# The last tile's y read straight from four PSUM banks, and the integers of the tile before it made by ScalarE alone

## The chip, the cores and the metric

One core of one Trainium2 chip runs the kernel. The metric is device microseconds of one execution. The kernel before took 420.11 us (median of 3 runs, 419.92 to 420.31). One execution was also recorded by the hardware profiler.

## The reference, cut to what matters

2048 tokens of 512 values pass through two residual blocks. The first sends each token through one of four expert MLPs. The second, with which this case deals, is a BitNet feed-forward layer: activations are rounded to 8-bit integers with one scale per token, weights are -1, 0 or 1, and a Hadamard transform stands before the down projection.

```
def act_quant(x):                       # per token: scale from the largest |x| of its row
    scale = 128 / clip(max(|x|, axis=-1), 1e-5)
    return clip(round(x * scale), -128, 127) / scale
gate, up = bitlinear(x, w_gate), bitlinear(x, w_up)
intermediate = silu(gate) * up          # 2048 values per token
y = fwht(intermediate)                  # Hadamard transform of the 2048 values
x = x + tanh(g) * bitlinear(y, w_down)  # y goes through act_quant first
```

The scale of a token needs the maximum over its whole row of y, so no integer of y can be made before the last part of that row is there.

## The kernel before, in words

The tokens form 16 tiles of 128 (NT = 16). A tile's 2048 values of y are worked on in NQ = 4 quarters of 512, one PSUM bank each. For one tile the steps are:

- gate and up products on TensorE, silu on ScalarE, their product on VectorE;
- four butterfly levels on VectorE (lines 1201 and 1209), which leave `mixed`;
- per quarter: four transposes on TensorE (line 427), ScalarE copies them from PSUM into `mT` (`mT_evacuate`, line 836), four Hadamard products on TensorE (line 588) leave y in a bank, ScalarE copies it into the SBUF tensor `y` (`y_evacuate`, line 841);
- VectorE takes the maximum of |y| and from it the scale `yqs`;
- integers: ScalarE writes `y8` (int8, which rounds) and widens it into `yq` (bf16); lines 824 and 829 in the loop, `end_integers` (892 and 896) at the end. VectorE can do the same in two passes (`y_integers`, lines 1364 and 1367);
- the DMA queue of SyncE (SP) transposes each quarter of `yq` into `yqT` (`turn_y`, lines 279 to 284), TensorE multiplies it by the down weights (line 595), VectorE scales and adds the residual (`finish`, line 1309), and GpSimd (POOL) writes the tile to the output by an indirect DMA (line 410).

The work on a tile is spread over several rounds of a loop. What remains after the loop is in a function `drain` on each engine, with an order written out by hand. It calls the last four tiles Z, A, B and C (12 to 15). In this text "B1" is quarter 1 of tile B, and so on. SP, POOL and the compute engines run in order, and each waits on semaphores that the others count up.

In the drain before: B's integers come half from VectorE (quarters 0 and 1, counted by `yq_end_set`) and half from ScalarE (2 and 3, counted by `yq_end_act`). C's four Hadamard quarters go in turn to the two banks `end_had`, and each waits until ScalarE has copied an earlier y out of its bank; VectorE then takes C's maximum quarter by quarter from SBUF (line 1410). C's integers are made by VectorE (0 and 2) and ScalarE (1 and 3). C's quarters are not transposed by DMA but by TensorE (`y_transposes`, line 693, called T0 to T3 here), and copied to `yT_end` by VectorE (line 1419) and ScalarE (line 935). TensorE's order at the end is C's Hadamards, A1, A2, A3, B0, B1, T0, T1, B2, T2, B3, T3, and the 16 products of C (line 681). A quarter of B can be transposed into `yqT` only after the product of the same quarter of A has read it:

```
sp.wait_ge(down_done, (t - 1) * NQ + (m + 1))
```

Of the kernel before, what the change touches and what calls it, by code (L numbers as in the profile page):

```python
# [22 lines left out]
ALU = mybir.AluOpType  # L23
ACT = mybir.ActivationFunctionType
# [7 lines left out]
NT = T // P  # L32
# [43 lines left out]
def gated_moe_bitnet_kernel(nc, x, ids, ctxt, wgate, wup, wdown, gates, consts, out):  # L76
    with ExitStack() as persistent:
# [123 lines left out]
        end_had = (ps_had, ps_up[0])  # L201
        first_h, first_xT = (ps_h, bank[4]), (ps_xT, bank[5])
        first_gate, first_up = (bank[7], bank[4]), (bank[5], bank[6])
        ps_down_last, ps_yT = bank[0], (bank[2], bank[5], bank[3], bank[4])


        in_ids, in_small, in_gate = sem("in_ids"), sem("in_small"), sem("in_gate")
# [39 lines left out]
        @block.sync  # L247
        def _(sp):
            sp.dma_start(idt[:, :], ids).then_inc(in_ids, 16)
            sp.dma_start(cst[:, 0:C_RANK], consts[:, 0:C_RANK]).then_inc(in_rank, 16)  # L250
            sp.dma_start(cst[:, C_RANK:C_N], consts[:, C_RANK:C_N]).then_inc(in_small, 16)
            sp.dma_start(gate_in[:, :], gates).then_inc(in_gate, 16)
            for e in range(E):
                if e == E - 1:
                    sp.wait_ge(gathered[1], 16)
                sp.dma_start(stage[:, e, :], ctxt[:, e, :]).then_inc(in_slot[e], 16)

            for w in range(3):
                for c in range(4):
                    if w == 0:  # L260
                        sp.wait_ge(ct_lo_set, c + 1)
                        sp.wait_ge(h_done, FIRST)
                    else:
                        sp.wait_ge(wround_set, 4 * (w - 1) + c + 1)
                    sp.dma_start(stage[:, c, :], W_DRAM[w][:, c, :]).then_inc(in_slot[c], 16)

            sp.wait_ge(wround_set, 9)

            def turn_x(t):
                sp.wait_ge(xq_set, t + 1)  # L270
                if t >= 1:
                    sp.wait_ge(gate_done, NQ * (t - 1) + 1)
                if t >= 2:
                    sp.wait_ge(up_done, NQ * (t - 1))
                sp.dma_start_transpose(xqT[:, t % 2, :, :], xq[:, t % 2, :]).then_inc(xqT_set, 16)

            def turn_y(t, m):
                if t == NT - 2:
                    sp.wait_ge((yq_end_set, yq_end_act)[m // 2], m % 2 + 1)
                else:  # L280
                    sp.wait_ge(yq_set, t * NQ + (m + 1))
                if t >= 1:
                    sp.wait_ge(down_done, (t - 1) * NQ + (m + 1))
                sp.dma_start_transpose(yqT[:, m, :, :], yq[:, t % 2, 512 * m:512 * (m + 1)]).then_inc(yqT_set[m], 16)

            turn_x(0)
            for t in range(NT + 1):
                if t == 3:
                    turn_x(4)
                if t >= 4:  # L290
                    turn_y(t - 4, 3)
                if t >= 3:
                    turn_y(t - 3, 0)
                    turn_y(t - 3, 1)
                if t != 3 and t + 1 < NT:
                    turn_x(t + 1)
                if t >= 3:
                    turn_y(t - 3, 2)
            turn_y(NT - 3, 3)
            for m in range(NQ):  # L300
                turn_y(NT - 2, m)
# [122 lines left out]
        def _(pe):  # L424
# [207 lines left out]
            def drain():  # L632

                Z, A, B, C = NT - 4, NT - 3, NT - 2, NT - 1

                def mix(n):
                    if n >= 2:
                        pe.wait_ge(mT_set, B * NQ + n - 1)
                    mix_transposes(B, B % 2, n)

                def had_b(n):
                    pe.wait_ge(y_set, B * NQ + n - 1)
                    hadamard(B, n, end_had[n % 2])

                mix(0)
                mix(1)
                down_product_int(Z, Z % 2, 1)
                had_b(0)
                down_product_int(Z, Z % 2, 2)
                had_b(1)  # L650
                mix(2)
                mix(3)
                down_product_int(Z, Z % 2, 3)
                had_b(2)
                had_b(3)
                pe.wait_ge(res_set, A - 1)
                down_product_int(A, A % 2, 0)
                for n in range(2):
                    pe.wait_ge(mT_set, B * NQ + n + 3)
                    last_transposes(n)  # L660
                for n in range(NQ):
                    pe.wait_ge(y_set, B * NQ + n + 3)
                    hadamard(C, n, end_had[n % 2])
                    if n < 2:
                        last_transposes(n + 2)
                for m in range(1, NQ):
                    down_product_int(A, A % 2, m)
                pe.wait_ge(res_set, B - 1)
                down_product_int(B, B % 2, 0)
                down_product_int(B, B % 2, 1)  # L670
                y_transposes(0)
                y_transposes(1)
                down_product_int(B, B % 2, 2)
                y_transposes(2)
                down_product_int(B, B % 2, 3)
                y_transposes(3)
                for m in range(NQ):
                    pe.wait_ge((yT_dve_set, yT_act_set)[m % 2], m // 2 + 1)
                    for g in range(4):
                        block_ = (m + 2) % NQ * 4 + g  # L680
                        last = nc.tensor.matmul(ps_down_last[:, :], yT_end[:, m, g, :],  # L681
                                                wq[:, 2, block_ * D:(block_ + 1) * D],
                                                start=(m == 0 and g == 0), stop=(m == 3 and g == 3))
                last.then_inc(down_done, NQ)

            def y_transposes(m):

                if m == 0:
                    pe.wait_ge(ident_set, 1)
                pe.wait_ge((yq_end_set, yq_end_act)[m % 2], 2 + m // 2 + 1)  # L690
                for g in range(4):
                    cols = slice(512 * m + g * P, 512 * m + (g + 1) * P)
                    last = nc.tensor.matmul(ps_yT[m][:, g * P:(g + 1) * P], yq[:, (NT - 1) % 2, cols], ident_bf[:, :],
                                            start=True, stop=True)
                last.then_inc(yT_done, 1)
# [14 lines left out]
        def _(act_e):  # L710
# [172 lines left out]
            def end_integers(t, m, i):  # L883

                b = t % 2
                if i % 2 == 0:
                    act_e.wait_ge(yqs_set, t + 1)
                if i < 2:
                    act_e.wait_ge(yq_set, (NT - 2) * NQ)
                else:  # L890
                    act_e.wait_ge(yq_end_act, i - 1)
                nc.scalar.activation(y8[:, i % 2, :], y[:, b, 512 * m:512 * (m + 1)], ACT.Copy,
                                     scale=yqs[:, b:b + 1]).then_inc(yround_set, 1)
                act_e.wait_ge(yround_set, (NT - 2) * NQ + i + 1)
                act_e.wait_ge(yqT_set[m], t * 16 - 16)
# [3 lines left out]
            def drain():  # L899
# [20 lines left out]
                mT_evacuate(C, 0)  # L920
                mT_evacuate(C, 1)
                integers(A, 3)
                y_evacuate(C, C % 2, 0, end_had[0])
                mT_evacuate(C, 2)
                y_evacuate(C, C % 2, 1, end_had[1])
                mT_evacuate(C, 3)
                end_integers(B, 2, 0)
                y_evacuate(C, C % 2, 2, end_had[0])
                end_integers(B, 3, 1)
                y_evacuate(C, C % 2, 3, end_had[1])  # L930
                end_integers(C, 1, 2)
                end_integers(C, 3, 3)
                for m in (1, 3):
                    act_e.wait_ge(yT_done, m + 1)
                    nc.scalar.activation(yT_end[:, m, :, :].rearrange("p g t -> p (g t)"), ps_yT[m][:, :],
# [15 lines left out]
        def _(dve):  # L951
# [409 lines left out]
            def y_integers(t, b, m):  # L1361

                quarter = y[:, b, 512 * m:512 * (m + 1)]
                st.did(ts(quarter, quarter, yqs[:, b:b + 1], MAGIC, ALU.mult, ALU.add))
                st.wait()
                dve.wait_ge(yqT_set[m], t * 16 - 16)
                ts(yq[:, b, 512 * m:512 * (m + 1)], quarter, MAGIC, QB - 1, ALU.subtract,
                   ALU.min).then_inc(yq_end_set, 1)
# [11 lines left out]
            def drain():  # L1380
# [19 lines left out]
                y_max(B, B % 2, 0, (0, 2), st)  # L1400
                step = y_max(B, B % 2, 1, (2, 4), st)
                end_scales(B, step, 2)
                dve.wait_ge(yqs_set, B + 1)
                for m in range(2):
                    y_integers(B, B % 2, m)
                finish(Z, Z % 2)
                for p in range(NQ):
                    dve.wait_ge(y_set, C * NQ + p + 1)
                    n = p
                    step = st.did(nc.vector.tensor_reduce(ymax_part[:, c, p:p + 1], y[:, c, 512 * n:512 * (n + 1)],  # L1410
                                                          AX_X, ALU.max, apply_absolute_value=True))
                end_scales(C, step, NQ)
                dve.wait_ge(yqs_set, C + 1)
                for m in (0, 2):
                    y_integers(C, c, m)
                finish(A, A % 2)
                for m in (0, 2):
# [97 lines left out]
```

## Time and profile before

| what | value |
|---|---|
| median of 3 runs | 420.11 us (419.92 to 420.31) |
| the profiled execution | 419.76 us, of which the span 417.8 us |
| TensorE matmul busy | 388.4 us (93% of the span) |
| VectorE busy | 365.6 us (88%) |
| ScalarE busy | 291.3 us (70%) |
| granted TensorE clock, mean | 0.995 |

The span goes from the first to the last instruction; 1.96 us of the profiled execution lie around it. The shares are means over stages with different limits. The change touches only the drain, which starts at about 380 us of the span, so what matters is who waits for whom between 390 and 411 us.

### The profile page before, as it was taken

Reading aid. Unit: us, or ns where it says so; the run is one execution under the profiler, and the core shown is the slowest. Engines: PE = TensorE matmul, PEld = TensorE weight load, DVE = VectorE, ACT = ScalarE, POOL = GpSimd, SP = SyncE. Lnnn points to the kernel's source line nnn. Section 1 sums busy time; section 2 is a strip of 40 time slices with the busy share of each in tenths; the row PEclk is TensorE's granted clock in tenths of the full one; section 3 lists DMA queues with packets and bytes.
Section 4 is the critical chain, followed back from the end, with each engine's and each line's share of the span. In section 5 each row is a group of like instructions: output and inputs, shape, how many; then the busy total and the mean of one; then the engine's idle time right before and its main releaser. Section 6 shows DMA issues by size and latency. Waiting matters only on the chain.

```text
span 417.8 us, 7359 instructions
## 1 busy us (share of the span) xinstructions
PE 388.4 (93%) x2170; PEld 270.2 (65%) x2203; DVE 365.6 (88%) x653; ACT 291.3 (70%) x450; POOL 175.3 (42%) x207
## 2 busy tenths in 40 slices
PE   1899999999999989989999999999999999999891
PEld 1347788888887564756666666666666666667740
DVE  6788587779888889999999999999999999998970
ACT  4446686587875243658888888888888888877960
POOL 0667310114124111053575575575575575522021
PEclk9999999999999999999999999999999999999997
DMA  7759474065000000235155155155155155255241
GB/s 244 268 160 417 154 247 157 1 211 192 2 15 0 13 14 8 57 63 103 44 109 126 44 107 126 44 107 126 43 107 126 43 107 126 48 106 113 50 102 50
DMA packets 48969, 43.66 MB, mean 105 GB/s; under 512 B 42673, under 2 KB 42801, under 8 KB 46897
## 3 DMA queue, kind: packets, MB, share of 16 engines
q1 hardware_dynamic: 44224, 27.11, 22.6%
q0 software_dynamic: 4720, 16.26, 16.5%
q8 instruction: 13, 0.21, 0.2%
q14 instruction: 12, 0.09, 0.1%
HBM read 21.33 MB, written 4.19 MB: 61 GB/s over the span
## 4 chain that ended last, share of the span: by engine, by line
PE 78%; DVE 11%; issue 5%; DMA 3%; ACT 2%; POOL 1%; DVEq 0%; SPq 0%; POOLq 0%; ACTq 0%
PE bank L465 21%; PE bank L588 13%; PE bank L595 11%; PE bank L564 10%; PE bank L571 10%; PE bank L427 9%; DVE prod L1182 2%; DVE ct_lo L972 1%; DMA xs<-x_dram,order 1%; PE bank L532 1%; DMA yqT<-yq 1%; PE bank L681 1%; DVE bfly L1209 1%; DVE mixed L1209 1%; DVE xs L1100 1%
## 5 line engine op out<-in xcount | busy, mean ns | idle before, releaser
L588 PEld LDWEIGHTS bank<-cst,mT 128*128 128x128 f32 x512 | 66.5, 191 | 12.9 <-issue 2.1
L588 PE MATMUL bank<-cst,mT 128*128 128x128 f32 x512 | 67.7, 276 | 3.4 <-ACT mT L836 3.4
L571 PE MATMUL bank<-wq,xqT 128*128 128x512 bf16 x232 | 61.0, 379 | 0.4
L595 PE MATMUL bank<-wq,yqT 128*128 128x512 bf16 x227 | 59.3, 379 | 1.6 <-DMA yqT<-yq 0.8
L564 PE MATMUL bank<-wq,xqT 128*128 128x512 bf16 x231 | 59.8, 379 | 0.5
L836 ACT ACTIVATE mT<-bank 128x512 f32<-128x512 f32 x64 | 37.6, 592 | 17.9 <-PE bank L427 17.9
L410 POOL DMA_INDIRECT out_dram<-res,order x16 | 19.4, 1215 | 70.4 <-DVE res L1309 70.4
L824 ACT ACTIVATE y<-y,yqs 128x512 int8<-128x512 f32 x56 | 40.2, 718 | 11.8 <-POOL yqs L368 11.8
L841 ACT ACTIVATE y<-bank 128x512 f32<-128x512 f32 x64 | 37.6, 588 | 9.7 <-PE bank L588 9.5
L861 ACT ACTIVATE sg<-bank,gate_s 128x512 f32<-128x512 f32 x60 | 41.0, 683 | 4.1 <-PE bank L564 3.9
L1182 DVE TENSOR_TENSOR prod<-bank,sg 128x512 f32<-128x512 f32 x64 | 43.3, 677 | 0.6 <-ACT sg L861 0.5
L571 PEld LDWEIGHTS bank<-wq,xqT 128*128 128x128 bf16 x240 | 23.5, 98 | 28.3
L427 PE MATMUL bank<-cst,mixed 128*128 128x128 f32 x256 | 37.9, 273 | 0.5 <-DVE mixed L1201 0.5
L427 PEld LDWEIGHTS bank<-cst,mixed 128*128 128x128 f32 x256 | 31.4, 141 | 10.5 <-issue 0.9
L1288 DVE TENSOR_REDUCE ymax_part<-y 128x1 f32<-128x1024 f32 x30 | 36.3, 1212 | 2.1 <-ACT y L841 1.0
L1209 DVE TENSOR_TENSOR mixed<-prod 128x1024 f32<-128x1024 f32 x32 | 37.8, 1219 | 0.1
L366 POOL TENSOR_SCALAR out_s<-yamax,down_c 128x1 f32<-128x1 f32 x13 | 29.7, 2282 | 19.3 <-DVE yamax L1299 19.3
L1209 DVE TENSOR_TENSOR prod<-bfly 128x1024 f32<-128x1024 f32 x30 | 36.0, 1211 | 0.0
L829 ACT ACTIVATE yq<-y 128x512 bf16<-128x512 int8 x56 | 35.3, 630 | 0.6
L1209 DVE TENSOR_TENSOR bfly<-prod 128x1024 f32<-128x1024 f32 x30 | 35.3, 1216 | 0.0
L595 PEld LDWEIGHTS bank<-wq,yqT 128*128 128x128 bf16 x240 | 23.2, 98 | 17.3 <-DMA yqT<-yq 1.5
L564 PEld LDWEIGHTS bank<-wq,xqT 128*128 128x128 bf16 x240 | 23.2, 98 | 16.3 <-ACT sg L861 0.8
(154 smaller groups left out, 806.4 us busy)
## 6 DMA issues: line engine op xcount, KB each, us to landing
mixed<-mixed POOLq DMA_DIRECT2D x15, 512.0 KB, 5.3
stage<-ctx_dram SPq DMA_DIRECT2D x4, 1024.0 KB, 7.7
stage<-wgate_dram SPq DMA_DIRECT2D x4, 1024.0 KB, 8.1
stage<-wup_dram SPq DMA_DIRECT2D x4, 1024.0 KB, 4.7
stage<-wdown_dram SPq DMA_DIRECT2D x4, 1024.0 KB, 4.7
yqT<-yq SPq DMA_TRANSPOSE x60, 2.4
cst<-consts_dram SPq DMA_DIRECT2D x1, 274.0 KB, 2.9
xs<-x_dram,order POOLq DMA_INDIRECT x16, 4.4
```

What stands on the lines that cost most here:

```text
L427: last = nc.tensor.transpose(bank_[:, c * P:(c + 1) * P], src(c), ident)
L465: last = nc.tensor.matmul(bank_[:, :], l[:, cols], r[:, ds(e * DC + c), :], start=(c == 0 and n == 0), stop=(c == DC - 1 and n == 2))
L564: last = nc.tensor.matmul(ps_gate[:, :], xqT[:, b, c, :], wq[:, 0, c * F + 512 * n:c * F + 512 * (n + 1)], start=(c == 0), stop=(c == DC - 1))
L571: last = nc.tensor.matmul(ps_up[n % 2][:, :], xqT[:, b, c, :], wq[:, 1, c * F + 512 * n:c * F + 512 * (n + 1)], start=(c == 0), stop=(c == ...
L588: last = nc.tensor.matmul(bank_[:, c * P:(c + 1) * P], mT[:, n % 2, c, :], had, start=True, stop=True)
L595: last = nc.tensor.matmul(ps_down[b][:, :], yqT[:, m, g, :], wq[:, 2, block_ * D:(block_ + 1) * D], start=(m == 0 and g == 0), stop=(m == ...
L824: nc.scalar.activation(y8[:, m % 2, :], y[:, b, 512 * m:512 * (m + 1)], ACT.Copy, scale=yqs[:, b:b + 1]).then_inc(yround_set, 1)
L836: nc.scalar.activation(mT[:, n % 2, :, :].rearrange("p c m -> p (c m)"), ps_mT[n % 2][:, :], ACT.Copy).then_inc(mT_set, 1)
L841: nc.scalar.activation(y[:, b, 512 * n:512 * (n + 1)], bank_[:, :], ACT.Copy).then_inc(y_set, 1)
L861: nc.scalar.activation(sg[:, n % 2, :], ps_gate[:, :], ACT.Silu, scale=gate_s[:, b:b + 1]).then_inc(sg_set, 1)
L1182: tt(prod[:, b, 4 * n:4 * n + 4, :].rearrange("p c m -> p (c m)"), up[n % 2][:, :], sg[:, n % 2, :], ALU.mult).then_inc(prod_set, 1)
L1209: return tt(dst[:, :, half], src[:, :, 0], src[:, :, 1], ALU.subtract if half else ALU.add)
```

## The change

Four parts, all in the drain:

1. C's four Hadamard quarters go to four different banks, `last_had` = banks 0, 2, 4 and 1. The first two are the banks of gate and up, no longer in use by then, and are not waited for; the other two wait for ScalarE's copies of B2 and B3. ScalarE's four copies of C's y are gone. VectorE takes the maximum from the banks, and the integers of C are made from the banks. T0 to T3 and the last product move to other banks.
2. All four quarters of B's integers are made by ScalarE, in order, after its last `mT_evacuate`; VectorE's two are gone, and `turn_y` for B waits for `yq_end_act` alone.
3. Of C's integers, ScalarE makes quarter 1 and VectorE 0, 2 and 3.
4. On VectorE `finish` of tile Z follows the scales of B directly.

```
-        ps_down_last, ps_yT = bank[0], (bank[2], bank[5], bank[3], bank[4])
+        last_had = (bank[0], bank[2], ps_had, ps_up[0])
+        ps_down_last, ps_yT = last_had[2], (bank[5], bank[3], last_had[0], last_had[1])
...
                 if t == NT - 2:
-                    sp.wait_ge((yq_end_set, yq_end_act)[m // 2], m % 2 + 1)
+                    sp.wait_ge(yq_end_act, m + 1)
...
                 for n in range(NQ):
-                    pe.wait_ge(y_set, B * NQ + n + 3)
-                    hadamard(C, n, end_had[n % 2])
+                    if n >= 2:
+                        pe.wait_ge(y_set, B * NQ + n + 1)
+                    hadamard(C, n, last_had[n])
                     if n < 2:
                         last_transposes(n + 2)
...
-                pe.wait_ge((yq_end_set, yq_end_act)[m % 2], 2 + m // 2 + 1)
+                if m == 1:
+                    pe.wait_ge(yq_end_act, NQ + 1)
+                else:
+                    pe.wait_ge(yq_end_set, (1, 0, 2, 3)[m])
...
-                nc.scalar.activation(y8[:, i % 2, :], y[:, b, 512 * m:512 * (m + 1)], ACT.Copy,
+                src = last_had[m][:, :] if t == NT - 1 else y[:, b, 512 * m:512 * (m + 1)]
+                nc.scalar.activation(y8[:, i % 2, :], src, ACT.Copy,
                                      scale=yqs[:, b:b + 1]).then_inc(yround_set, 1)
...
                 integers(A, 3)
-                y_evacuate(C, C % 2, 0, end_had[0])
                 mT_evacuate(C, 2)
-                y_evacuate(C, C % 2, 1, end_had[1])
                 mT_evacuate(C, 3)
-                end_integers(B, 2, 0)
-                y_evacuate(C, C % 2, 2, end_had[0])
-                end_integers(B, 3, 1)
-                y_evacuate(C, C % 2, 3, end_had[1])
-                end_integers(C, 1, 2)
-                end_integers(C, 3, 3)
+                for m in range(NQ):
+                    end_integers(B, m, m)
+                end_integers(C, 1, NQ)
...
-                st.did(ts(quarter, quarter, yqs[:, b:b + 1], MAGIC, ALU.mult, ALU.add))
+                st.did(ts(quarter, last_had[m][:, :], yqs[:, b:b + 1], MAGIC, ALU.mult, ALU.add))
...
                 end_scales(B, step, 2)
-                dve.wait_ge(yqs_set, B + 1)
-                for m in range(2):
-                    y_integers(B, B % 2, m)
                 finish(Z, Z % 2)
-                for p in range(NQ):
-                    dve.wait_ge(y_set, C * NQ + p + 1)
-                    n = p
-                    step = st.did(nc.vector.tensor_reduce(ymax_part[:, c, p:p + 1], y[:, c, 512 * n:512 * (n + 1)],
+                for n in range(NQ):
+                    dve.wait_ge(had_done, C * NQ + n + 1)
+                    step = st.did(nc.vector.tensor_reduce(ymax_part[:, c, n:n + 1], last_had[n][:, :],
                                                           AX_X, ALU.max, apply_absolute_value=True))
                 end_scales(C, step, NQ)
                 dve.wait_ge(yqs_set, C + 1)
-                for m in (0, 2):
+                for m in (0, 2, 3):
                     y_integers(C, c, m)
```

ScalarE's order in the drain before, from A3's integers on (`y<-bank4` and `y<-bank1` copy C's y; `y8` and `yq` are the two passes of a quarter's integers, the first two quarters B's and the last C1):

```order
L836 ACTIVATE mT<-bank3 128x512 [waits had_done,mT_done]
L841 ACTIVATE y<-bank1 128x512 [waits had_done]
L836 ACTIVATE mT<-bank5 128x512 [waits had_done,mT_done]
L892 ACTIVATE y8<-y,yqs 128x512 [waits yq_set,yqs_set]
L896 ACTIVATE yq<-y8 128x512 [waits yqT_set2,yround_set]
L841 ACTIVATE y<-bank4 128x512 [waits had_done]
L892 ACTIVATE y8<-y,yqs 128x512 [waits yq_set]
L896 ACTIVATE yq<-y8 128x512 [waits yqT_set3,yround_set]
L841 ACTIVATE y<-bank1 128x512 [waits had_done]
L892 ACTIVATE y8<-y,yqs 128x512 [waits yq_end_act,yqs_set]
L896 ACTIVATE yq<-y8 128x512 [waits yqT_set1,yround_set]
```

The same place now (line numbers are those of the changed kernel):

```order
L841 ACTIVATE mT<-bank3 128x512 [waits had_done,mT_done]
L841 ACTIVATE mT<-bank5 128x512 [waits had_done,mT_done]
L898 ACTIVATE y8<-y,yqs 128x512 [waits yq_set,yqs_set]
L902 ACTIVATE yq<-y8 128x512 [waits yqT_set0,yround_set]
L898 ACTIVATE y8<-y,yqs 128x512 [waits yq_set]
L902 ACTIVATE yq<-y8 128x512 [waits yqT_set1,yround_set]
L898 ACTIVATE y8<-y,yqs 128x512 [waits yq_end_act]
L902 ACTIVATE yq<-y8 128x512 [waits yqT_set2,yround_set]
L898 ACTIVATE y8<-y,yqs 128x512 [waits yq_end_act]
L902 ACTIVATE yq<-y8 128x512 [waits yqT_set3,yround_set]
L898 ACTIVATE y8<-bank2,yqs 128x512 [waits yq_end_act,yqs_set]
L902 ACTIVATE yq<-y8 128x512 [waits yqT_set1,yround_set]
```

The copies of y are gone, four pairs for B stand in a row behind the last `mT`, and C1 comes fifth.

VectorE's order in the drain before, behind the scales of B (`res` is `finish` of tile Z):

```order
L1364 TENSOR_SCALAR y<-y,yqs 128x512 [waits yqs_set]
L1367 TENSOR_SCALAR yq<-y 128x512 [waits yqT_set0,dve_step]
L1364 TENSOR_SCALAR y<-y,yqs 128x512
L1367 TENSOR_SCALAR yq<-y 128x512 [waits yqT_set1,dve_step]
L1309 SCALAR_TENSOR_TENSOR res<-bank6,out_s,xs 128x512 [waits res_free,down_done]
L1410 TENSOR_REDUCE ymax_part<-y 128x1 [waits y_set] x4
```

The same place now:

```order
L1310 SCALAR_TENSOR_TENSOR res<-bank6,out_s,xs 128x512 [waits res_free,down_done]
L1407 TENSOR_REDUCE ymax_part<-bank0 128x1 [waits had_done]
L1407 TENSOR_REDUCE ymax_part<-bank2 128x1 [waits had_done]
L1407 TENSOR_REDUCE ymax_part<-bank4 128x1 [waits had_done]
L1407 TENSOR_REDUCE ymax_part<-bank1 128x1 [waits had_done]
```

Z's `finish` and C's maximum moved up by B's four integer passes, and the maximum waits for TensorE instead of ScalarE.

## Rows read from the trace of the kernel before

**Rows 1.** The page's engines: busy us (share of the span) xinstructions.

```profile
PE 388.4 (93%) x2170; PEld 270.2 (65%) x2203; DVE 365.6 (88%) x653; ACT 291.3 (70%) x450; POOL 175.3 (42%) x207
```

**Rows 2.** The chain of waits from C's Hadamards on: start us, us, what.

```profile
394.17 0.89 PE bank L588 x8
...
395.50 1.96 PE bank L588 x16
...
398.41 3.55 DMA yqT<-yq
...
402.00 1.04 PE bank L595 x4
403.04 0.45 PE bank L693 x8
...
409.15 0.76 DVE res L1309
...
410.70 0.97 POOL out_dram L410
```

**Rows 3.** Waits from 394 us on: who waited <- for whom, us, times, longest.

```profile
PE bank L595 <- DMA yqT<-yq: 0.8, 1, 0.8
```

**Rows 4.** The DMAs issued in four stretches: 396 to 397.5, 397 to 398.5, 391 to 393, 301.6 to 301.8.

```profile
yqT<-yq SPq DMA_TRANSPOSE x1, 3.9
...
q8 instruction: 1, 0.02, 5.4%
...
yqT<-yq SPq DMA_TRANSPOSE x1, 2.3
...
out_dram<-res,order POOLq DMA_INDIRECT x1, 3.6
yqT<-yq SPq DMA_TRANSPOSE x1, 3.4
```

**Rows 5.** Timeline: the output write and the transpose issued behind it, in the loop.

```profile
300.91 1.29 POOL L410 DMA_INDIRECT out_dram<-res,order  x1 [3.38 <-DVE res L1309]
...
301.67 1.20 SPq L284 DMA_TRANSPOSE yqT<-yq  x1
```

**Rows 6.** Timeline of the drain: start us, us, engine, line, operation [idle before <-releaser].

```profile
395.10 0.48 DVE L1364 TENSOR_SCALAR y<-y,yqs 128x512 f32<-128x512 f32 x1
...
395.60 0.60 ACT L836 ACTIVATE mT<-bank 128x512 f32<-128x512 f32 x1
...
396.07 0.72 ACT L892 ACTIVATE y<-y,yqs 128x512 int8<-128x512 f32 x1
...
396.82 0.74 DVE L1309 SCALAR_TENSOR_TENSOR res<-bank,out_s,xs 128x512 f32<-128x512 f32 x1
...
397.48 1.86 DVE L1410 TENSOR_REDUCE ymax_part<-y 128x1 f32<-128x512 f32 x3
397.52 3.66 PE L595 MATMUL bank<-wq,yqT 128*128 128x512 bf16 x15
...
398.41 1.09 POOL L410 DMA_INDIRECT out_dram<-res,order  x1 [17.33 <-DVE res L1309]
...
399.73 0.69 DVE L1410 TENSOR_REDUCE ymax_part<-y 128x1 f32<-128x512 f32 x1 [0.39 <-ACT y L841]
...
401.41 0.72 ACT L892 ACTIVATE y<-y,yqs 128x512 int8<-128x512 f32 x1 [1.71 <-DVE yqs L1377]
401.42 0.48 DVE L1364 TENSOR_SCALAR y<-y,yqs 128x512 f32<-128x512 f32 x1
...
402.17 0.63 ACT L896 ACTIVATE yq<-y 128x512 bf16<-128x512 int8 x1
402.28 0.48 DVE L1364 TENSOR_SCALAR y<-y,yqs 128x512 f32<-128x512 f32 x1
...
402.70 0.71 ACT L892 ACTIVATE y<-y,yqs 128x512 int8<-128x512 f32 x1
```

**Rows 7.** VectorE by line and shape from 280 us on: busy us, mean ns.

```profile
L1419 DVE CAST yT_end<-bank 128x512 bf16<-128x512 f32 x2 | 1.4, 686 | 0.1
```

More of the change, by code:

```diff
@@ L885, in end_integers @@
                 b = t % 2
-                if i % 2 == 0:
+                if i in (0, NQ):
                     act_e.wait_ge(yqs_set, t + 1)
```

## Prediction

> **What bounds the kernel now.** I read the page first: TensorE is busy for 93% of the span, the other engines for less [rows 1]. A change of the drain can therefore only win where TensorE stands still there, or where work is taken from its path. The chain of waits shows where that is. From C's Hadamards to the output it stays on TensorE with one break: the Hadamard quarters C2 and C3 run to 395.50 + 1.96 = 397.46 us, A1 follows, then come 3.55 us of the DMA that transposes B1 (398.41 to 401.96), and B1's product at 402.00 [rows 2]. From there TensorE has no further gap until `finish` of C at 409.15 and the last output write at 410.70. The view of waits prices the break: TensorE stood idle for 0.8 us before B1, for the DMA [rows 3]. The timeline agrees: A1, A2, A3 and B0 run from 397.52 for 3.66 us (15 of 16 products are recorded), to 401.18, and B1 begins 0.82 us later [rows 6].
>
> That DMA could not start earlier, because A1 had to free its buffer first. And it was slow: a transpose that runs alone lands 2.3 us after its issue, this one took 3.55 [rows 2, 4]. The timeline says what lay beside it: the output write of tile Z was issued at 398.41 as well [rows 6]. In the loop the same pair stands: a write at 300.91, a transpose 0.76 us behind it at 301.67, and the transpose lands after 3.4 us, the write after 3.6 [rows 4, 5]. So a transpose next to an output write is about 1.1 us late. The Trainium skill, "DMA: Bandwidth & Descriptors", section "Queues, rings and completion order", says that each DMA engine takes turns between the queues that have work for it; by that rule the transpose shares with the write, and the trace agrees (3.4 against 2.3).
>
> **The change part by part.**
>
> *C's y stays in four banks.* ScalarE's four copies go. On TensorE's path they matter only through the waits in front of C's Hadamards. One quarter takes 0.89 us, two took 1.96 instead of 1.78 [rows 2]: at most 0.18 us to win. C3 must still wait for its transposes, which end at 395.50, and for ScalarE's `mT` copy of 0.60, which began at 395.60 behind a copy of y [rows 2, 6]. It can now begin at about 395.54. I take 0.05 us, so the Hadamards end at 397.42; the bounds are 0 and 0.18. The banks of C0 and C1 cost no wait, since gate and up are long done with them.
>
> *VectorE.* B's four integer passes go; Z's `finish` begins at 395.10, where the first of them stood, instead of 396.82, and ends at 395.84 [rows 6]. The maxima begin 0.66 us behind its start (397.48 - 396.82), at 395.76, 0.62 us each (1.86 / 3). The fourth must wait for C3 (397.42) and starts at about 397.6 instead of 399.73. From the fourth maximum to the first integer pass took 1.69 us (399.73 to 401.42) [rows 6], so C's integers begin at 399.3 instead of 401.42. No maximum from a bank is in the trace. Reading SBUF in 0.62 us is the lower bound, `finish` from a bank in 0.74 the upper one, which adds up to 0.5 us if all four grow; I take 0.62. An integer quarter took 0.86 us (402.28 - 401.42). Its first pass now reads a bank: 0.48 as before at least, 0.74 at most, and I take the 0.69 of the cast from a bank, the nearest row [rows 6, 7]. So a quarter costs 1.07 us: C0 is ready at 400.5, C2 at 401.5, C3 at 402.6. TensorE wants T0 after 402, T2 at 404 and T3 at 405, so all this is hidden. Without that cover C3's quarter would cost 1.07 us. `finish` of A and the two casts follow until 404.7, before the products that need them (405 and 407).
>
> *ScalarE.* Its integers of B begin behind the last `mT`, 0.47 us after that one's start as before (396.07 - 395.60): at 396.01. A pair of passes takes 1.29 us from start to start (402.70 - 401.41), and its `yq` is done 0.76 + 0.63 = 1.39 us after its start [rows 6]. So B0 is ready at 397.40, B1 at 398.69, B2 at 399.98, B3 at 401.27, and C1, which starts at 401.17 and has long had its scale, at 402.56. C1 is the one of C's quarters that can hold TensorE: T1 not before 402.6. The bounds of a pair are 1.29 and, with no overlap at all, 0.72 + 0.63 + two waits of 0.04 = 1.43.
>
> *The DMAs.* SP's queue is in order: A3, B0, B1, B2, B3. B0's wait is new: the row queued behind it is B1, and TensorE waits for both. Issues now come at 397.45, 398.74, 400.03 and 401.32 (the above plus 0.05). At 2.3 us they land at 399.8, 401.05, 402.35, 403.6. A1 frees B1's buffer at 398.3, before the 398.74, so that wait is gone, and ScalarE is what is late next. But Z's output write moves too. It was issued 0.85 us after `finish` ended (397.56 to 398.41); that gives 396.69. B0's transpose comes 0.76 us behind it, exactly the distance in the loop. I take the 3.4 us of that row, not the 2.3: B0 lands at 400.85.
>
> *The sum.* One quarter's product takes 0.87 us (3.66 / 4, less the 0.18 by which the last one's end is longer: 1.04 against 0.86). TensorE ends A3 at 397.42 + 3 x 0.87 = 400.03, waits 0.87 us for B0 (start 400.9), ends it after 1.04 at 401.94 and B1 at 402.81 (landed 401.1). What follows is unchanged: 409.15 - 403.04 = 6.11 us from the end of B1 to `finish` of C [rows 2]; T1, B2 and B3 find their data. End 408.92 instead of 409.15, a gain of 0.23 us. The stall has moved from B1 to B0 and kept its size; what is won is that it ends a little earlier. The profiled execution took 419.76 us (span 417.8), and would take 419.53; the median of the runs shown lies 0.35 above it, so **419.9 us** on that scale. A measurement of this kernel can tell about 0.2%, 0.84 us, from no change.
>
> **The rivals.**
>
> *No collision.* If the write and B0 don't disturb each other, B0 lands at 399.8 and TensorE goes on to T1, which waits for ScalarE until 402.6. From there 0.40 for T1 with its end and 5.66 (6.11 less the 0.45 of T0 and T1): 408.66, that is -0.5 us, 419.6. For it speaks only that the write might be issued later; against it the loop's rows.
>
> *Nothing gained.* B0's transpose took 3.9 us before, with Z's write issued only near its end; between 397 and 398.5 an instruction fetch of 0.02 MB fell into its time [rows 4]. If B0 is caught by both, it lands at 401.35 or later, and the end is 409.4: +0.3, 420.4. Against it: that fetch lies in the stretch before 398.5, and B0's transpose is now issued 1.3 us later than before, so most of its time lies behind the fetch. The Trainium skill, "Runtime: NRT & Kernel Launch", "Instruction fetch mechanics", says an engine's instructions are refilled in blocks of 256; by that the fetch stays at its place in the program, near 397.3, and would miss B0.
>
> *Slower: ScalarE becomes the bound.* Five pairs stand in a row in front of T1. With a pair of p us T1 starts at 396.15 + 5p and the end is 402.21 + 5p. It equals today's end at p = 1.39 and is 0.84 us slower from p = 1.56. At the unoverlapped 1.43 it is 409.36, +0.2; at 1.6, +1.1 (421.2). For it: five times 1.29 is all in the chain. Against: the rows show the overlap.
>
> *Faster beyond 0.84 us.* All of the Hadamards' 0.18, no stall at all (0.82 with the 0.18 of restart): 1.2 us at most, 418.9. It would need C1 before 402.2, against ScalarE's chain.
>
> **How the numbers follow.** Forecast (-0.6 to +0.2) 0.45; no collision 0.2; nothing gained 0.17; ScalarE the bound 0.1, half of it beyond 0.84 us; faster beyond 0.84 us 0.08. The first three all lie within 0.2%. With the scatter of the runs (0.2 us each way) this gives faster 0.12, same 0.78, slower 0.10. The range goes from 419.1 to 420.7: the no-collision end less half a microsecond, the nothing-gained end plus the scatter.
>
> **What would show it right or wrong.** In the profile after: Z's output write at about 396.7; B0's transpose issued near 397.45 and landing after 3.3 us or more; TensorE idle for 0.6 to 0.9 us before B0 and not before B1; C's scale done 2 us earlier (399.3) with T0, T2 and T3 never waited for; ScalarE's pairs 1.29 us apart, from 396.0. The prediction is wrong if TensorE waits at T1 for ScalarE, if a maximum or integer pass from a bank takes over 1 us, or if the copies were worth more on the Hadamards than 0.18.

## Result: 0.2% slower, with the stall in front of B3

The changed kernel takes **421.03 us** (median of 14 runs, 420.12 to 421.35); the kernel before, on the same chip, 420.11 us (14 runs). The ratio is 1.002, 95% interval 1.0012 to 1.0028: slower by 0.92 us, where 0.2 us less was forecast. It lies outside the range of 419.1 to 420.7. The profiled execution took 420.69 us (span 418.5), one of the shorter ones; that of the kernel before took 419.76.

The profile's engine row hardly differs from [rows 1]: TensorE is busy for 1.7 us more, and 33 more of its records are kept, so nothing follows from that.

```profile
PE 390.1 (93%) x2203; PEld 270.1 (65%) x2203; DVE 365.5 (87%) x651; ACT 290.7 (69%) x448; POOL 175.4 (42%) x207
```

The chain of waits from B1's transpose on shows what bounds the end now (start us, us, what):

```profile
398.76 2.40 DMA yqT<-yq
...
401.42 3.68 DMA yqT<-yq
...
405.14 1.04 PE bank L596 x4
406.18 0.22 PE bank L698 x4
406.40 3.47 PE bank L683 x16
...
409.90 0.76 DVE res L1310
...
411.45 0.98 POOL out_dram L411
```

In [rows 2] the DMA in the chain was B1's transpose and TensorE followed it without a gap. Here it is B3's, which is issued at 401.42 and takes 3.68 us. Behind it `finish` of C begins at 409.90 instead of 409.15, and the last write at 411.45 instead of 410.70: 0.75 us later.

The waits from 394 us on show two stalls where [rows 3] had one (0.8 before B1), and a small one for ScalarE's C1:

```profile
PE bank L596 <- DMA yqT<-yq: 1.4, 2, 1.1
...
PEld bank L698 <- ACT yq L902: 0.2, 1, 0.2
```

The timeline of the drain answers to [rows 6]:

```profile
395.01 0.74 DVE L1310 SCALAR_TENSOR_TENSOR res<-bank,out_s,xs 128x512 f32<-128x512 f32 x1
...
395.36 2.07 PE L589 MATMUL bank<-cst,mT 128*128 128x128 f32 x16
395.56 0.60 ACT L841 ACTIVATE mT<-bank 128x512 f32<-128x512 f32 x1 [0.73 <-PE bank L428]
...
396.05 0.71 ACT L898 ACTIVATE y<-y,yqs 128x512 int8<-128x512 f32 x1
396.60 1.09 POOL L411 DMA_INDIRECT out_dram<-res,order  x1 [15.61 <-DVE res L1310]
...
399.16 0.75 DVE L1365 TENSOR_SCALAR y<-bank,yqs 128x512 f32<-128x512 f32 x1
...
400.33 1.93 PE L596 MATMUL bank<-wq,yqT 128*128 128x512 bf16 x8 [0.31 <-DMA yqT<-yq]
...
401.85 0.63 ACT L902 ACTIVATE yq<-y 128x512 bf16<-128x512 int8 x1
...
405.14 1.04 PE L596 MATMUL bank<-wq,yqT 128*128 128x512 bf16 x4 [1.13 <-DMA yqT<-yq]
```

Up to 402 us almost everything but B0 is where the prediction put it: the Hadamards end at 397.43 (395.36 + 2.07), the last `mT` starts at 395.56, Z's `finish` starts at 395.01, its write at 396.60, ScalarE's pairs at 396.05, C's integers at 399.16. TensorE waits 0.31 us before B0 and nothing before B1. Then it stands still for 1.13 us before B3. The DMA view of two stretches, 396 to 398 and 402 to 403, says what lay beside the transposes (the last number is the us from issue to landing):

```profile
out_dram<-res,order POOLq DMA_INDIRECT x1, 3.0
yqT<-yq SPq DMA_TRANSPOSE x1, 2.7
...
q8 instruction: 1, 0.02, 8.0%
...
yqT<-yq SPq DMA_TRANSPOSE x1, 3.7
```

B0's transpose lies beside Z's write and takes 2.7 us, not 3.4. Into B3's falls an instruction fetch of 0.02 MB, which starts at 402.42. In the kernel before, that fetch came at 397.22, in B0's transpose [rows 4], where 3.9 us cost TensorE no wait before B0. The fetch has moved by 5.2 us, from a transpose with time to spare to the one that TensorE needs next.

### The profile page after: what moved, and what is told of

Its sections match the earlier page's. It is cut to its first block, busy times and chain, and to the rows that moved or that the text cites. A ratio compares the mean times of both kernels' runs of the same rounds, so it can differ in the third digit from the quotient of the medians.

```text
span 418.5 us, 7386 instructions
## 1 busy us (share of the span) xinstructions
PE 390.1 (93%) x2203; PEld 270.1 (65%) x2203; DVE 365.5 (87%) x651; ACT 290.7 (69%) x448; POOL 175.4 (42%) x207
## 4 chain that ended last, share of the span: by engine, by line
PE 77%; DVE 11%; issue 5%; DMA 3%; ACT 2%; POOL 1%; DVEq 0%; SPq 0%; POOLq 0%; ACTq 0%
PE bank L466 21%; PE bank L589 12%; PE bank L596 11%; PE bank L572 10%; PE bank L565 10%; PE bank L428 9%; DVE prod L1183 2%; DMA yqT<-yq 1%; DMA xs<-x_dram,order 1%; DVE ct_lo L973 1%; PE bank L533 1%; PE bank L683 1%; DVE bfly L1210 1%; DVE mixed L1210 1%; DVE xs L1101 1%
## 5 line engine op out<-in xcount | busy, mean ns | idle before, releaser
L596 PE MATMUL bank<-wq,yqT 128*128 128x512 bf16 x240 | 61.2, 379 | 1.4 <-DMA yqT<-yq 1.4
L565 PE MATMUL bank<-wq,xqT 128*128 128x512 bf16 x240 | 61.6, 379 | 0.0
L572 PE MATMUL bank<-wq,xqT 128*128 128x512 bf16 x240 | 61.6, 379 | 0.0
L846 ACT ACTIVATE y<-bank 128x512 f32<-128x512 f32 x60 | 35.3, 589 | 9.8 <-PE bank L589 9.6
```

The source lines that it names most:

```text
L565: last = nc.tensor.matmul(ps_gate[:, :], xqT[:, b, c, :], wq[:, 0, c * F + 512 * n:c * F + 512 * (n + 1)], start=(c == 0), stop=(c == DC - 1))
L572: last = nc.tensor.matmul(ps_up[n % 2][:, :], xqT[:, b, c, :], wq[:, 1, c * F + 512 * n:c * F + 512 * (n + 1)], start=(c == 0), stop=(c == ...
L596: last = nc.tensor.matmul(ps_down[b][:, :], yqT[:, m, g, :], wq[:, 2, block_ * D:(block_ + 1) * D], start=(m == 0 and g == 0), stop=(m == ...
```

## The experiments

My theory: the moved fetch costs the time, and without it the prediction's sum holds. Against it stood that the change itself is slower (five pairs on ScalarE, passes from banks), and that any added work on TensorE changes the time for another reason. "Fetch" below is the start of the last instruction fetch of 0.02 MB; B0 to B3 are the us from issue to landing of the four transposes; "tail" is the time from the end of C's Hadamards to the last output write, read from the one profiled execution. The ratios are from runs taken side by side on one chip, and are not the quotients of two medians.

| kernel | fetch | B0, B1, B2, B3 | TensorE waits before | tail | median us | ratio to before (95%) |
|---|---|---|---|---|---|---|
| before | 397.22 | 3.94, 3.55, 2.65, 2.33 | B1 0.83 | 13.23 | 420.11 | |
| after | 402.42 | 2.75, 2.41, 2.35, 3.68 | B0 0.31, B3 1.13 | 14.02 | 421.03 | 1.0020 (1.0012 to 1.0028) |
| after + 12 products | 393.81 | 3.38, 2.60, 2.35, 2.33 | B0 0.95 | 13.09 | 419.26 | 0.9990 (0.9981 to 0.9999) |
| after + 24 products | 393.81 | 3.34, 2.56, 2.36, 2.33 | B0 0.90 | 13.05 | 419.42 | 0.9991 (0.9982 to 1.0000) |
| after + 48 products | 392.00 | 3.39, 2.61, 2.35, 2.33 | B0 0.96 | 13.10 | 419.24 | 0.9988 (0.9973 to 1.0002) |
| after + 2 waits | 397.03 | 3.15, 2.41, 2.34, 2.33 | B0 0.72 | 12.86 | 419.39 | 0.9995 (0.9986 to 1.0004) |
| before + 12 products | 396.60 | 3.15, 3.35, 2.39, 2.33 | B1 0.88 | 13.04 | 419.37 | 0.9988 (0.9975 to 1.0002) |

### Both kernels once more

No edit, one execution each, to see whether the fetch comes at the same place again.

> The changed kernel once more, unaltered, for a second trace. Theory F (fetch): the loss comes from TensorE's wait of 1.1 us before B3, and that wait from an instruction fetch of 0.02 MB that falls into B3's transpose. Then again a fetch lies between 401 and 403 us and B3's transpose takes 3.3 us or more (3.7 in the first trace), B0's 2.4 to 2.8. Rival S (ScalarE's row of pairs): B3 is late because it is handed over last, at 401.4, and its transpose is slow there whatever else runs; then it is as slow in a trace whose fetch lies elsewhere.

> The kernel before once more, unaltered, for a second trace. F: the fetch lies near 397.3 again (B0's transpose 3.9 us, but TensorE needs B0 only at 400.1, so it costs next to nothing), none between 400 and 404, and B2 and B3 take 2.3 to 2.6. S says nothing of this kernel. If the fetch lies elsewhere by several us in the same program, its place is chance and the loss cannot be a fixed property of the change.

The DMA view of the changed kernel, 402.3 to 404 (its whole drain is 0.9 us later here), and its wait:

```profile
q8 instruction: 1, 0.02, 5.7%
...
yqT<-yq SPq DMA_TRANSPOSE x1, 4.0
...
PE bank L596 <- DMA yqT<-yq: 1.7, 2, 1.4
```

And of the kernel before, 395.5 to 397.5:

```profile
q8 instruction: 1, 0.02, 4.7%
...
yqT<-yq SPq DMA_TRANSPOSE x1, 4.2
```

The fetch came at 403.33 and at 397.04, again within B3's transpose in one kernel and B0's in the other. In both executions of the kernel before it starts when 2144 of TensorE's 2203 weight loads have begun, in both of the changed kernel when 2167 have. So, as far as two executions of each show, its place belongs to the program, not to the execution. In the second trace of the kernel before TensorE does wait 0.36 us before B0, and then 0.55 before B1. (The two times, 421.85 and 419.57, are single ones.)

### Products on TensorE, far ahead of the drain

The results of these products are read by nothing; they stand near 4 us, where TensorE has idle time, and only make its program longer. N is 12, 24 and 48.

```diff
+            for _ in range(N):
+                nc.tensor.matmul(bank[7][:, 0:64], tri_bf, m, start=True, stop=True)
```

> The changed kernel with 24 extra small products on TensorE in its idle time near 4 us (their results are not used), so that every later instruction of TensorE lies 48 instructions further back in its program. F, if the fetches are TensorE's: the fetch comes 24 products earlier, near 397 to 399 instead of 402.5; B3's transpose lands 2.3 to 2.5 us after its issue, TensorE does not wait before B3, and the time falls by 0.8 to 1.2 us, to 419.8 to 420.2, that is 0.998 to 1.000 of the kernel before. S: nothing moves, 421.0, ratio 1.002.

> The changed kernel with 12 extra small products in TensorE's idle time near 4 us instead of 24. Theory F: the time follows from where the instruction fetch falls among B's transposes. The fetch comes somewhere between its places in the two kernels measured (393.9 with 24 extra products, 402.5 with none). If it falls on B0's transpose (397.5 to 400), B0 lands after 3.9 us or more, TensorE waits 1.2 to 2 us before it, and the time is 419.8 to 420.6; if on B3's, 420.7 to 421.3 as unshifted; if on none, 419.4. Rival E (the 24 extra products gain by themselves, by warming the clock or by another start of the program): 12 of them give about half of the 1.6 us, 420.2, wherever the fetch falls and with B3's wait as it was.

> The changed kernel with 48 extra small products near 4 us. F: the fetch comes 24 products or more earlier than with 24 extra, before 393 us, where no transpose that TensorE waits for is in flight; no wait before B3, B0 waits 0.3 to 0.9 us beside the output write of Z, 419.2 to 419.7, as with 24. E: twice the gain, 418 or less. If the 48 products (about 3 us) don't fit into the 3.8 us of idle time, the whole program starts later by what is over.

All three move the fetch to before B0's transpose is issued, with 24 to 393.81 where 397 to 399 was expected. It falls into A2's transpose (3.87, 3.86 and 2.97 us), for which nobody waits. With 24, the DMA view of three stretches (393.5 to 394.3, 397.4 to 397.8, 401.4 to 402) and the timeline:

```profile
q8 instruction: 1, 0.02, 8.2%
...
out_dram<-res,order POOLq DMA_INDIRECT x1, 3.2
yqT<-yq SPq DMA_TRANSPOSE x1, 3.3
...
yqT<-yq SPq DMA_TRANSPOSE x1, 2.3
```

```profile
395.37 2.07 PE L591 MATMUL bank<-cst,mT 128*128 128x128 f32 x16
...
396.79 1.08 POOL L411 DMA_INDIRECT out_dram<-res,order  x1 [15.61 <-DVE res L1312]
...
397.47 1.20 SPq L285 DMA_TRANSPOSE yqT<-yq  x1
...
400.94 1.89 PE L598 MATMUL bank<-wq,yqT 128*128 128x512 bf16 x8 [0.90 <-DMA yqT<-yq]
```

B3's transpose is back at 2.3 us, nobody waits for it, and the only stall is the forecast one: 0.90 us before B0 (0.87 forecast), start 400.94 (400.9 forecast). The last write begins at 410.49, in these two executions 0.21 us ahead of before's 410.70 (0.23 forecast). The gain does not grow with the number of products: 12, 24 and 48 give 0.9990, 0.9991 and 0.9988. This speaks against the products' own work as the reason, and for the place of the fetch.

### The same products in the kernel before

> The kernel before, with the same 12 extra small products near 4 us. Theory F: the fetch leaves 397.2 for a place ahead of 395; B0's transpose lands 2.4 us after its issue instead of 3.9 to 4.2, but TensorE needs B0 only at 400.1, so at most 0.3 us is won, and the wait of 0.8 us before B1 stays (beside Z's output write): 419.6 to 420.1, ratio 0.999 to 1.000. Rival E' (the extra products make any kernel faster, by their effect on the start or on the loop): 0.7 to 1.6 us faster here too, ratio 0.996 to 0.998.

```profile
q8 instruction: 1, 0.02, 20.4%
...
yqT<-yq SPq DMA_TRANSPOSE x1, 3.1
...
PE bank L597 <- DMA yqT<-yq: 0.9, 1, 0.9
```

These are its DMA view from 396.4 to 396.8, and its wait. The fetch was expected before 395 and moved by 0.6 us only, to 396.60, into A3's transpose (4.43 us) and B0's (3.15 us); the wait before B1 stayed. The kernel took 0.32 us less, not distinguishable from none, while after gained 1.3 us against before by the same edit (from +0.92 to -0.42). So the products are not worth 1.3 us by themselves. But beside this run the changed kernel with the same products gains nothing that could be told: ratio 0.9990 against 0.9988, tail 13.09 against 13.04. The 0.19 us by which this tail is shorter than that of the kernel before is B1's transpose: 3.35 us here, 3.55 there (3.54 in the second trace), where the fetch was still running when B1 was issued and B0 landed late through it. So part of the stall that the prediction meant to win back was the fetch's, and that the change by itself wins 0.2 us is not shown.

### Two waits put back on TensorE

The change took two wait instructions out of TensorE's program, those in front of C0's and C1's Hadamards. Here they stand again, for counts that are reached by then (the trace shows no wait for them):

```diff
-                    if n >= 2:
-                        pe.wait_ge(y_set, B * NQ + n + 1)
+                    pe.wait_ge(y_set, B * NQ + (n + 3 if n < 2 else n + 1))
```

> The changed kernel with the two waits that it took from TensorE's program put back in front of C0 and C1. They wait for ScalarE's copies of B2 and B3, which are there already, so they cost nothing but two instructions, and TensorE's program has as many as the kernel before. If these two instructions are what moved the fetch from 397.2 (kernel before, two traces) to 402.5 to 403.4 (changed kernel, two traces), the fetch is back near 397, B3 lands 2.3 us after its issue, and the time is 419.2 to 420.0, ratio 0.998 to 1.000 (B0 may be later than 400.3 because of the fetch). If the fetch follows TensorE's progress or its waits for data instead, it stays at T1, B3 takes 3.3 us or more, and the time is 420.7 to 421.3.

The DMA view from 396.9 to 397.3 and from 401.2 to 401.6, then the timeline:

```profile
q8 instruction: 1, 0.02, 15.0%
...
out_dram<-res,order POOLq DMA_INDIRECT x1, 3.2
yqT<-yq SPq DMA_TRANSPOSE x1, 3.2
...
yqT<-yq SPq DMA_TRANSPOSE x1, 2.3
```

```profile
396.56 1.09 POOL L411 DMA_INDIRECT out_dram<-res,order  x1 [15.61 <-DVE res L1309]
...
397.30 1.22 SPq L285 DMA_TRANSPOSE yqT<-yq  x1
...
400.59 1.89 PE L596 MATMUL bank<-wq,yqT 128*128 128x512 bf16 x8 [0.72 <-DMA yqT<-yq]
```

This is the sharpest of the runs. Nothing differs from the changed kernel but two waits that never wait. The fetch returns to 397.03, again when 2144 weight loads have begun, B3's transpose to 2.3 us, and the ratio from 1.0020 to 0.9995 (0.9986 to 1.0004). So the fetch's place hangs on TensorE's program, and the loss of the change on the place at which its two instructions fewer leave the fetch.

### Two of B's integers back on VectorE

C's y stays in its banks; VectorE makes B0's and B1's integers ahead of Z's `finish`, as before, and ScalarE those of B2, B3 and C1.

```diff
-                for m in range(NQ):
-                    end_integers(B, m, m)
-                end_integers(C, 1, NQ)
+                end_integers(B, 2, 0)
+                end_integers(B, 3, 1)
+                end_integers(C, 1, 2)
...
                 end_scales(B, step, 2)
+                dve.wait_ge(yqs_set, B + 1)
+                for m in range(2):
+                    y_integers(B, B % 2, m)
                 finish(Z, Z % 2)
```

> The changed kernel with one part undone: VectorE makes the integers of B0 and B1 again, ahead of Z's finish, and ScalarE only those of B2, B3 and C1. C's y stays in four banks. S: ScalarE hands over B3 near 398.7, its transpose is issued near 401 as in the kernel before and everything is given back: 419.9 to 420.2, ratio 0.999 to 1.000, with TensorE waiting 0.8 us before B1 as in the kernel before. F: the same if the fetch misses the transposes of B; if the fetch still falls at 402 to 403, B3 (issued near 401, landing at 403.4 undisturbed) is late by 0.5 to 1.2 us again and the time stays at 420.5 to 421.

It took 420.19 us, ratio 1.0003 (0.9993 to 1.0012): as before. Its waits, and the DMA view from 405.5 to 406:

```profile
PE bank L596 <- DMA yqT<-yq: 0.9, 1, 0.9
...
PE bank L683 <- DVE yT_end L1419: 0.3, 1, 0.3
...
q8 instruction: 1, 0.02, 12.0%
```

Z's write is late again and meets B1, whose transpose took 3.35 us: the old stall is back. The fetch comes at 405.62, behind B3's landing. This run tells little of the change itself, because it moved the fetch too; its profiled execution, 421.61, is a long one, so its end is not compared.

### Z's write out of the way, and C's integers on one engine

With the 24 products, VectorE's `finish` of Z is moved ahead of B's maxima:

```diff
+                finish(Z, Z % 2)
                 y_max(B, B % 2, 0, (0, 2), st)
...
-                finish(Z, Z % 2)
```

> The 24 extra products, and on VectorE the finish of tile Z moved up once more, in front of B's maxima, so that Z's output write is issued near 393.3 instead of 396.7. Theory Z (the write delays B0's transpose, 3.3 us against 2.35): B0 lands at 399.9 to 400.0, TensorE does not wait before it, the next limit is T1, which waits for ScalarE's C1 until 402.6; TensorE ends 0.2 to 0.4 us earlier than with the 24 products alone, 419.0 to 419.3. Rival: ScalarE starts B's integers later, because B's scale comes 0.74 us later on VectorE (395.7 instead of 395.0); the scale is needed at 396.05 only, but if it decides, the time is 0.0 to 0.3 us longer.

```profile
392.71 1.09 POOL L411 DMA_INDIRECT out_dram<-res,order  x1 [12.27 <-DVE res L1312]
```

The timeline has Z's write at 392.71. No transpose of B collides: 2.37, 2.38, 2.35 and 2.32 us. (A2's and A3's, beside the write and the fetch, take 4.44 and 3.44 us, and nobody waits for them.) The last write begins at 409.42, 12.72 us behind the end of C's Hadamards. TensorE does not wait before B0, and 0.17 us before B1. 419.06 us, ratio 0.9983 (0.9972 to 0.9994), an interval that overlaps that of the 24 products alone. What is late next is ScalarE's C1 (0.3 us before T1). So VectorE, which has time, then takes all of C's integers, and ScalarE the copies of T0 and T1:

```diff
-                end_integers(C, 1, NQ)
-                for m in (1, 3):
+                for m in (0, 1):
...
-                for m in (0, 2, 3):
+                for m in range(NQ):
                     y_integers(C, c, m)
```

> The kernel with the early finish of Z and the 24 products, and in addition all four quarters of C's integers on VectorE in order; ScalarE makes B's alone and copies T0 and T1, VectorE T2 and T3. If ScalarE's C1 is what T1 waits for, TensorE goes on at 402.2 instead of 402.6, until B3 (landing at 403.8) stops it: 0.1 to 0.4 us earlier than the kernel with the early finish, 418.7 to 419.1, ratio to the kernel before 0.996 to 0.998. Against: VectorE makes C3 at 403.4 and finishes A behind it, so its copies of T2 and T3 may come too late for the last products; then the same or 0.3 us longer.

It is the fastest kernel here: **418.31 us** against 419.68, less than expected, ratio 0.9965 (0.9952 to 0.9978). Without the 24 products, the same kernel:

> The kernel with Z's early finish and all of C's integers on VectorE, without the extra products. If the fetch stays with the place at which it fell in the changed kernel (the start of T1, now near 401.8), it falls on the transposes of B2 (issued 399.9) or B3 (issued 401.2): one of them lands after 3.3 to 4 us, TensorE waits up to 1.2 us, and the time is 419.0 to 419.9. If the fetch came there only because TensorE stood at T1's wait, it falls elsewhere and the time is that with the products, 418.3 to 418.9.

```profile
q8 instruction: 1, 0.02, 25.3%
...
yqT<-yq SPq DMA_TRANSPOSE x1, 4.0
...
405.12 1.04 PE L596 MATMUL bank<-wq,yqT 128*128 128x512 bf16 x4 [1.70 <-DMA yqT<-yq]
```

Its DMA view from 401.9 to 402.3 and the timeline show the fetch (402.05) in B3's transpose again, 4.03 us, and 1.70 us of stall, more than expected: 420.38 us, ratio 1.0012 (0.9999 to 1.0026). The two kernels differ in 24 unused products near 4 us, and in 2.07 us of time. The run also settles a rival: in the changed kernel an output write is issued at 404.09, before B3 has landed, and could be what delays it; here that write is issued at 405.06, 0.02 us before B3 lands, and B3 is as late.

## Why the prediction was wrong

**The step that failed** is "T1, B2 and B3 find their data", and behind it "the fetch stays at its place in the program, near 397.3, and would miss B0". It did miss B0, but it did not stay. TensorE stood 1.13 us before B3, and 0.22 us before T1 for ScalarE's C1, which the prediction had named as a sign of being wrong. I weighed the fetch only at B0 and took its place as fixed. The change takes two waits out of TensorE's program, so its place was open, and B3 was a place where it would decide. By the working's own rates a fetch in B3's transpose (1.6 us more, as B0's 3.9 against 2.3) would have given 405.2 instead of 403.6 for its landing; TensorE wanted it at about 404.2, so the end would have come 1.0 us later.

**How much it was.** TensorE reached `finish` of C at 409.90, 0.98 us behind the 408.92 of the sum: 1.13 for B3, 0.56 back because B0 cost 0.31 and not 0.87, and about 0.4 for T1's wait for C1 (0.22) and for restarts. With the fetch elsewhere and nothing else changed but products that nobody reads, the tail was 0.13 to 0.18 us shorter than before's, 0.23 forecast. The agreement is partly luck: before's own tail held about 0.2 us of the fetch, and with the 12 products, which take that away, it is as short as the changed kernel's with products (13.04 against 13.05 to 13.10).

**The terms that held.** The Hadamards gained 0.04 us (0.05 forecast). ScalarE's pairs stand 1.27 to 1.28 us apart, so C1 was done at 402.48 (402.56 forecast). No integers of C that VectorE makes were waited for. The maxima and first passes, by line and shape:

```profile
L1407 DVE TENSOR_REDUCE ymax_part<-bank 128x1 f32<-128x512 f32 x4 | 2.5, 682 | 0.0
...
L1365 DVE TENSOR_SCALAR y<-bank,yqs 128x512 f32<-128x512 f32 x3 | 2.2, 745 | 0.0
```

A maximum from a bank costs what it costs from SBUF (682 ns against 678 in the kernel before), as taken; the first integer pass costs 0.745, the upper bound of 0.74, not the 0.69 taken, hidden either way.

**B0 and Z's write.** I took 3.4 us from a loop row in which the transpose follows the write by 0.76 us. With the products it followed by 0.68 us and took 3.34 to 3.39, as taken. In the changed kernel the distance was 397.45 - 396.60 = 0.85 and the transpose took 2.75 (2.74 in the second trace), so that B0 landed at 400.20 and not at 400.85. The longer distance alone does not explain it. In the loop of the same trace stands a pair 0.84 us apart (timeline, and DMA view from 364.2 to 364.4):

```profile
363.41 1.30 POOL L411 DMA_INDIRECT out_dram<-res,order  x1 [3.29 <-DVE res L1310]
...
364.25 1.19 SPq L285 DMA_TRANSPOSE yqT<-yq  x1
...
yqT<-yq SPq DMA_TRANSPOSE x1, 3.3
```

With the two waits B0's took 3.15 at 0.74, but there a fetch had begun 0.27 us before it as well. So the collision is real, and why it was 0.6 us smaller in the changed kernel is not shown.

**The rivals.** "Nothing gained" named the right cause, a transpose caught by the fetch, but at B0 and at +0.3. ScalarE as the bound did not come: its pairs were 1.28, far from 1.39. "No collision" holds for T1: with B0 nearly in time, TensorE did wait there for ScalarE.

**What the Trainium skill says of the fetch.** The Trainium skill, "Runtime: NRT & Kernel Launch", "Instruction fetch mechanics", has instructions refilled in blocks of 256 and calls the cost mostly hidden. That a fetch's place depends on the count of instructions agrees with the run of two waits. That it stays near its time, as the prediction drew from this, does not: two instructions moved it from 402.42 to 397.03. And where it is not hidden it cost 1.13 to 1.70 us of TensorE, through another queue's transpose. Between the last two fetches lie 140 and 142 recorded products in the two traces before, 166 and 163 in those after, so the time of a fetch cannot be counted off from the one before it.

**What stays open** is the rule by which the place moves. Twelve products moved the last fetch of after by 8.6 us and that of before by 0.6 us; 24 moved it no further than 12, 48 by 1.8 us more. In both traces of the changed kernel it comes just as T1 starts. No run here tells why. Open is also what the change is worth by itself: with the fetch out of the way in both kernels, nothing that these runs can tell. (The run of two waits has the shortest tail, 12.86, but its ratio, 0.9995, is not below 0.9988, that of before with 12 products.)

## What to carry to other kernels

Before crediting a change of a few tenths of a microsecond, look where the instruction fetches lie among the small transposes that the path waits for; a few instructions more or less on an engine can move one there. When a change turns out slower than its sum, compare those rows first and run the kernel again with its program shifted, before blaming the change. Shift the kernel before as well: it may hold some of the same cost. And where an output write stands beside a small transpose that the path waits for, try to move it well ahead: here a distance of 4.0 us instead of 0.7 took B0's transpose from 3.34 to 2.37 us, though the gain in time is too small to be told.

## What the runs showed of the hardware that was not expected

An instruction fetch of 0.02 MB took 0.9 to 1.7 us. In the 13 traces, from 230 us on, the 297 transposes of `yq` beside which neither such a fetch nor any DMA but another transpose was in flight took 2.30 to 2.38 us. All 16 in which a fetch began 1.0 to 2.1 us after the issue took 3.6 to 4.4 us. Behind a fetch that began 0.4 to 0.6 us before the issue, with no write beside it, they took 2.31 to 2.56 us. Two wait instructions that never wait moved a fetch from 402.42 to 397.03. A transpose 0.7 to 0.85 us behind an output write took 3.3 to 3.5 us in the loop where no fetch fell into it; in the changed kernel's drain it took 2.75, and no run shows why.
